# First loads from two queues in chunks of four batches, and masked values written by ScalarE straight from PSUM

## What is computed

```python
x = x + _L0_xattn_ref(_layernorm(x, axis=-1), ctx_768, wq, bq, wk, bk, wv, bv, wo, bo)
# in it, 16 heads of 8 features
q = (x @ wq + bq); k = (y @ wk + bk); v = (y @ wv + bv)
attn = softmax(q k^T / sqrt(8)); out = attn v
return out @ wo + bo
```

## Time and profile before

| | us |
|---|---|
| median of 3 runs | 555.57 (554.25 to 555.69) |
| the profiled execution | 554.04 |
| its span, from the first to the last instruction | 552.2 |
| TensorE busy in the span | 499.0 (90%) |
| VectorE / ScalarE / GpSimd busy | 397.7 / 269.5 / 254.7 |

### The profile page before, as it was taken

One profiled execution on the slowest core, in us unless ns is written; L12 is line 12 of the kernel. 1 busy time (PEld: TensorE's weight loads), 2 busy tenths in 40 slices (PEclk: granted clock), 3 DMA queues, 4 the chain that ended last, 5 costly groups with the idle time before them and its releaser, 6 DMA issues.

```text
span 552.2 us, 13385 instructions
## 1 busy us (share of the span) xinstructions
PE 499.0 (90%) x5113; PEld 380.0 (69%) x5113; DVE 397.7 (72%) x1065; ACT 269.5 (49%) x724; POOL 254.7 (46%) x345
## 2 busy tenths in 40 slices
PE   1698989788999998999989999899878899999996
PEld 1556666545667776877767877788646797798884
DVE  3578888757587789877897879978975578534443
ACT  1355564354476754556646567565543444413331
POOL 3877676215446425556255555334230980084400
PEclk9999999999999999999999999999999999999999
DMA  6900000000001101111000000022201200010001
GB/s 176 244 13 2 4 1 4 2 2 7 3 2 31 31 2 31 31 31 31 2 1 2 3 4 2 2 59 59 60 1 37 78 2 2 0 42 1 2 2 39
DMA packets 21807, 14.47 MB, mean 26 GB/s; under 512 B 5864, under 2 KB 21072, under 8 KB 21744
## 3 DMA queue, kind: packets, MB, share of 16 engines
q1 hardware_dynamic: 21744, 13.61, 9.3%
HBM read 12.30 MB, written 1.05 MB: 24 GB/s over the span
## 4 chain that ended last, share of the span: by engine, by line
PE 69%; DVE 21%; ACT 4%; issue 3%; DMA 1%; SPq 1%; POOL 0%; DVEq 0%; ACTq 0%
PE bank L1681 9%; PE bank L1296 6%; PE bank L1690 5%; PE bank L1452 4%; PE bank L1412 4%; PE bank L1365 4%; PE bank L1432 4%; PE bank L1459 4%; PE bank L1440 4%; PE bank L1621 4%; PE bank L1697 3%; PE bank L1423 3%; PE bank L1282 3%; ACT work L1025 2%; PE bank L1510 2%
## 5 line engine op out<-in xcount | busy, mean ns | idle before, releaser
L478 POOL TENSOR_TENSOR work<-work,rsum 128x496 f32<-128x496 f32 x64 | 64.1, 1014 | 131.1 <-DVE rsum L745 131.1
L1084 ACT ACTIVATE work<-bank,negmax 128x124 f32<-128x124 f32 x256 | 72.7, 378 | 78.5 <-DVE ipa_s L731 78.5
L513 POOL TENSOR_SCALAR work<-work,slot 128x128 f32<-128x128 f32 x64 | 49.8, 792 | 47.6 <-DVE slot L820 31.0
L959 DVE SCALAR_TENSOR_TENSOR work<-work,bank 128x256 f32<-128x256 f32 x64 | 26.9, 420 | 39.5 <-ACT work L1225 39.3
L1681 PE MATMUL bank<-work 128*128 128x256 f32 x224 | 53.5, 382 | 1.4 <-DVE work L962 1.4
L461 POOL TENSOR_TENSOR work<-work 128x512 f32<-128x512 f32 (+2 forms) x48 | 40.2, 837 | 14.1 <-DVE work L701 11.6
L737 DVE COPY work<-bank 128x512 f32<-128x512 f32 x64 | 43.6, 682 | 2.0 <-PE bank L1423 2.0
L1225 ACT ACTIVATE work<-bank 128x256 f32<-128x256 f32 x64 | 24.5, 384 | 41.2 <-PE bank L1681 30.2
L1681 PEld LDWEIGHTS bank<-work 128*128 128x128 f32 x224 | 40.3, 190 | 6.2 <-issue 1.6
L410 POOL TENSOR_TENSOR rstd<-veps,minus_half 128x1 f32<-128x1 f32 (+4 forms) x26 | 20.3, 781 | 51.7 <-DVE veps L555 51.7
L599 DVE TENSOR_REDUCE negmax<-bank 128x8 bf16<-128x1024 f32 x32 | 39.1, 1221 | 5.2 <-PE bank L1267 5.0
(11 more groups left out here) (196 smaller groups left out, 1106.7 us busy)
## 6 DMA issues: line engine op xcount, KB each, us to landing
work<-in_L_ffn_w_dram SPq DMA_DIRECT2D x42, 128.0 KB, 2.3
out_dram<-x_all SPq DMA_DIRECT2D x4, 256.0 KB, 2.5
x_all<-in_x_dram SPq DMA_DIRECT2D x1, 768.0 KB, 6.4
ctx_all<-in_L_ffn_w_dram SPq DMA_DIRECT2D x6, 128.0 KB, 2.2
ctx_all<-in_ctx_dram SPq DMA_DIRECT2D x1, 576.0 KB, 8.2
work<-in_L_xattn_Wq_dram SPq DMA_DIRECT2D x1, 512.0 KB, 8.9
...
```

The source lines that it names most:

```text
L478: pool.tensor_tensor(part, part, rsum1[:, b % 2, CH * n:CH * n + CH].unsqueeze(2).broadcast_to((128, CH, ORG)), ALU.mult).then_inc(Z.norm, 1)
L513: ins = pool.tensor_scalar(ohw_of(e)[:, k, :], count[:, :], slot[:, h, 0, k, e % E1:e % E1 + 1], slot[:, h, 1, k, e % E1:e % E1 + 1], ALU. ...
L1084: ins = act.activation(p1[:, b % 2, n, c, 0:ORG], blocks(bank[n])[:, c, 0:ORG], ACT.Exp, bias=negmax1[:, b % 2, CH * n + c:CH * n + c + 1])
```

## The change

It does three things in the first attention.

- **Loads.** x and context come in four chunks of four batches, in turn, on SyncE's queue, each with semaphores of its own. ScalarE issues the nine loads of the first attention's weights on its queue, in another order, before its table load; the six that the projections need count on a semaphore `qkv0`, the other three on `attn0`. The statistics go by four batches, in rounds -3, -2 and -1, and so do GpSimd's powers.
- **Products.** The two products leave the head of TensorE's program and stand behind round -3. VectorE takes them behind its round -3, and GpSimd adds the bias from round -2 on, behind the masks.
- **Masked values.** VectorE clears `vm0` once. ScalarE's copy of v goes from PSUM straight into the blocks of `vm0` that are not zero (`own_blocks`: 4 x 4 blocks of 8 columns per partition). `v0T` and GpSimd's multiply are gone; who waited for `v_sb` waits for `vm`.

```diff
@@ -106,14 +106,15 @@
-        work = Arena("work", 42000)
+        work = Arena("work", 42032)
         xn = sb("xn", [128, 2, D])
         xT = sb("xT", [128, 2, 128])
         cT_all = sb("cT_all", [C, B, 128])
         qm0 = work.take([128, 4, CH, 128])
         p0T = work.take([128, 2, CH, CH, 128])
-        vm0 = work.take([128, 5, CH, 128])
+        vm_flat = work.take([128, 5 * CH * 128 + 32])
+        vm0 = vm_flat[:, 0:5 * CH * 128].rearrange("p (s g n) -> p s g n", s=5, g=CH)
         km0 = work.take([128, 3, CH, 128], BF16)
...
@@ -283,6 +284,12 @@
+        def own_blocks(c):
+            at = CH * 128 * (c % 5)
+            wide = vm_flat[:, at:at + CH * (128 + D0)].rearrange("p (g n) -> p g n", g=CH)
+            return wide[:, :, 0:128].rearrange("p g (i n) -> p g i n", i=4)[:, :, :, 0:D0]
         def rw2_of(b):
...
@@ -323,20 +330,10 @@
         def _(sp):
-            def load(first, end, x_done, ctx_done):
-                sp.dma_start(x_all[:, first:end, :], T["x"][first:end, :, :].rearrange("b s d -> s b d")).then_inc(x_done, 16)
-                sp.dma_start(ctx_all[:, first:end, :], T["ctx_768"][first:end, :, :].rearrange("b s c -> s b c"))\
-                    .then_inc(ctx_done, 16)
-            load(0, 4, got.x0, got.ctx0)
-            sp.dma_start(wq0[:, :], T["L0_xattn_wq"]).then_inc(got.attn0, 16)
-            sp.dma_start(wk0[:, :], T["L0_xattn_wk"]).then_inc(got.attn0, 16)
-            for bias, name in ((bq0, "L0_xattn_bq"), (bk0, "L0_xattn_bk"), (bv0, "L0_xattn_bv")):
-                sp.dma_start(bias[:, :], T[name].rearrange("(p a) -> p a", a=1)).then_inc(got.attn0, 16)
-            sp.dma_start(wv0[:, :], T["L0_xattn_wv"]).then_inc(got.attn0, 16)
-            sp.dma_start(wo0[:, :], T["L0_xattn_wo"]).then_inc(got.attn0, 16)
-            sp.dma_start(gate_in[:, :], T["L0_ffn_gate_w"]).then_inc(got.attn0, 16)
-            sp.dma_start(bias0[:, :], T["L0_xattn_bo"].rearrange("(a n) -> a n", a=1).broadcast_to((128, D))).then_inc(got.attn0, 16)
-            load(4, B, got.x, got.ctx)
+            for n in range(4):
+                part = slice(4 * n, 4 * n + 4)
+                sp.dma_start(x_all[:, part, :], T["x"][part, :, :].rearrange("b s d -> s b d")).then_inc(x_in[n], 16)
+                sp.dma_start(ctx_all[:, part, :], T["ctx_768"][part, :, :].rearrange("b s c -> s b c")).then_inc(ctx_in[n], 16)
             for w, rows, name in ((wq1, D, "Wq"), (wk1, C, "Wk"), (wv1, C, "Wv")):
...
@@ -424,21 +421,17 @@
             pool.wait_ge(made.masks, 1)
-            pool.wait_ge(made.bias, 1)
             pool.wait_ge(made.cols, 2 * CH)
             def round0(b):
                 a, c = b + 4, b + 3
-                if b == -3:
-                    rstds(4, B)
+                if -3 <= b <= -1:
+                    rstds(4 * (b + 4), 4 * (b + 5))
                 if b == 0:
                     pool.wait_ge(A.cT, 4)
                     pool.tensor_copy(ctx_ipaT[:, :].rearrange("p (b j) -> p b j", b=B), cT_all[:, :, ORG:S]).then_inc(W.ctx, 1)
                 if b in (6, 10, 14):
                     rstds(b - 6, b - 2)
-                if there(a):
-                    pool.wait_ge(A.xn, a + 1)
-                    pool.tensor_tensor(x_all[:, a, :], x_all[:, a, :], bias0[:, :], ALU.add).then_inc(A.xb, 1)
                 if there(c):
...
@@ -448,10 +441,12 @@
                                        ALU.mult).then_inc(A.qm, 1)
-                    pool.wait_ge(A.v_sb, c + 1)
-                    after(pool, A.pv, c - 4)
-                    pool.tensor_tensor(vm0[:, c % 5, :, :], v0T[:, c % 2, :].unsqueeze(1).broadcast_to(wide0), own_col[:, :, :],
-                                       ALU.mult).then_inc(A.vm, 1)
+                if b == -2:
+                    pool.wait_ge(made.bias, 1)
+                for n in (0, 1, 2) if b == -2 else (a,) if b > -2 and there(a) else ():
+                    pool.wait_ge(A.xn, n + 1)
+                    pool.tensor_tensor(x_all[:, n, :], x_all[:, n, :], bias0[:, :], ALU.add).then_inc(A.xb, 1)
             def experts_sum(g):
...
@@ -561,7 +556,8 @@
                 return variances(ln.stats, end, first, end)
-            first_statistics(0, 4, got.x0)
+            dve.memset(vm_flat[:, :], 0.0).then_inc(made.vm, 1)
+            first_statistics(0, 4, x_in[0])
             dve.wait_ge(made.hmask, 3)
...
@@ -577,13 +573,22 @@
             xn0_of(0)
-            dve.wait_ge(got.attn0, 16 * 9)
-            dve.tensor_copy(bv0_wide[:, :], bv0[:, :].broadcast_to((128, 128))).then_inc(made.bias_w, 1)
-            dve.wait_ge(made.bias_p, 1)
-            dve.tensor_tensor(bias0[:, :], OUT0[:, 0:D], bias0[:, :], ALU.add).then_inc(made.bias, 1)
-            dve.wait_ge(F.gate_tr, 1)
-            dve.tensor_copy(gateT[:, :], MAX0[:, 0, 0:E0]).then_inc(F.gateT, 1)
+            def product_input():
+                dve.wait_ge(got.qkv0, 16 * 6)
+                dve.tensor_copy(bv0_wide[:, :], bv0[:, :].broadcast_to((128, 128))).then_inc(made.bias_w, 1)
+            def products_taken():
+                dve.wait_ge(got.attn0, 16 * 3)
+                dve.wait_ge(made.bias_p, 1)
+                dve.wait_ge(F.gate_tr, 1)
+                dve.tensor_tensor(bias0[:, :], OUT0[:, 0:D], bias0[:, :], ALU.add).then_inc(made.bias, 1)
+                dve.tensor_copy(gateT[:, :], OUT0[:, D:D + E0]).then_inc(F.gateT, 1)
             dve.wait_ge(made.consts, 2)
+            rstd_at = {}
...
@@ -612,8 +617,8 @@
                 n, m, t, y = b + 1, b + 2, b - 1, b - 2
-                if b == -3:
-                    rest = first_statistics(4, B, got.x)
+                if -3 <= b <= -1:
+                    rstd_at["first", b] = first_statistics(4 * (b + 4), 4 * (b + 5), x_in[b + 4])
                 if b < FILL:
...
@@ -637,8 +642,8 @@
                     dve_stats(dve, A, y)
-                if b == -3:
-                    dve.wait_ge(ln.rstd, rest)
+                if b <= -2 or b % 4 == 3 and b < 8:
+                    dve.wait_ge(ln.rstd, rstd_at["first", (b + 1) // 4 - 3] if b > -2 else 1)
                 if there(b + 5):
...
@@ -930,6 +934,10 @@
                 round0(b)
+                if b == -4:
+                    product_input()
+                if b == -3:
+                    products_taken()
                 if b in (5, 9, 13, 17):
...
@@ -998,14 +1006,23 @@
         def _(act):
+            for w, name in ((wk0, "wk"), (wq0, "wq"), (wv0, "wv")):
+                act.dma_start(w[:, :], T["L0_xattn_" + name]).then_inc(got.qkv0, 16)
+            for bias, name in ((bk0, "bk"), (bq0, "bq"), (bv0, "bv")):
+                act.dma_start(bias[:, :], T["L0_xattn_" + name].rearrange("(p a) -> p a", a=1)).then_inc(got.qkv0, 16)
+            act.dma_start(wo0[:, :], T["L0_xattn_wo"]).then_inc(got.attn0, 16)
+            act.dma_start(gate_in[:, :], T["L0_ffn_gate_w"]).then_inc(got.attn0, 16)
+            act.dma_start(bias0[:, :], T["L0_xattn_bo"].rearrange("(a n) -> a n", a=1).broadcast_to((128, D))).then_inc(got.attn0, 16)
             act.preload_act_table(ACT.Exp)
-            act.wait_ge(got.attn0, 16 * 9)
+            act.wait_ge(made.vm, 1)
             def round0(b):
                 a, c, n = b + 4, b + 3, b + 4
                 if n < 4:
                     act.wait_ge(A.ctx_tr, n + 1)
                     act.activation(cT_all[:, 4 * n:4 * n + 4, :], blocks(SC0[:, n, :], C), ACT.Copy).then_inc(A.cT, 1)
+                if c == 0:
+                    act.wait_ge(got.qkv0, 16 * 6)
                 if there(c):
...
@@ -1016,8 +1033,9 @@
                     act.activation(q0_bf[:, c % 3, :], TURN0[:, 128:256], ACT.Identity, bias=bq0[:, :]).then_inc(A.q_bf, 1)
-                    after(act, A.vm, c - 1)
-                    act.activation(v0T[:, c % 2, :], TURN0[:, 384:512], ACT.Copy).then_inc(A.v_sb, 1)
+                    after(act, A.pv, c - 4)
+                    act.activation(own_blocks(c), TURN0[:, 384:512].rearrange("p (i g d) -> p g i d", i=4, g=CH), ACT.Copy)\
+                        .then_inc(A.vm, 1)
                 if there(b):
...
@@ -1253,7 +1271,7 @@
-                pe.wait_ge(got.ctx0 if n == 0 else got.ctx, 16)
+                pe.wait_ge(ctx_in[n], 16)
                 for k in range(4):
...
@@ -1311,10 +1329,12 @@
                 after(pe, A.xT, min(a, B))
-                after(pe, A.v_sb, min(c, B))
+                after(pe, A.vm, min(c, B))
                 if there(a):
                     pe.wait_ge(A.xn, a + 1)
                     pe.transpose(TURN0[:, 0:128], xn_in[:, a % 3, :], ident[:, :]).then_inc(A.tr, 1)
+                if c == 0:
+                    pe.wait_ge(got.qkv0, 16 * 6)
                 if there(c):
...
@@ -1620,16 +1640,16 @@
                     mm.then_inc(Z.proj, 1)
-            pe.wait_ge(got.attn0, 16 * 9)
-            pe.wait_ge(made.bias_w, 1)
-            pe.matmul(OUT0[:, 0:D], bv0_wide[:, :], wo0[:, :], start=True, stop=True).then_inc(made.bias_p, 1)
```

(18 more changed lines are left out.)

9 lines of the change are left out of this document (4 added, 5 removed).

## The result

| | before | after |
|---|---|---|
| median of 4 runs, us | 555.63 (554.25 to 556.56) | 548.87 (548.65 to 549.96) |
| the profiled execution / its span, us | 554.04 / 552.2 | 549.04 / 547.3 |
| TensorE busy in the span, us | 499.0 (90%) | 501.2 (92%) |
| VectorE / ScalarE / GpSimd busy, us | 397.7 / 269.5 / 254.7 | 399.9 / 269.8 / 235.2 |

The ratio is 0.9888, with an interval from 0.9861 to 0.9915. The forecast was 549.3 us. The medians differ by 6.8 us, the two profiled executions by only 5.0, and that gap turns out to be worth a look.

The account below looks back on a forecast made before the run. The prediction took TensorE to bound the kernel nearly everywhere except the start-up, where late loads do; 6.45 - 0.35 + 0.2 = 6.3 us off the median of 555.57 gave 549.3 us, range 547.2 to 551.6.

Parts of the forecast that it names:

- Term 1: Start-up: with earlier loads, batch 0's projection starts at 9.4 instead of 15.85, 6.45 us earlier.
- the bound of 1.4 us for a locked-out GpSimd: Start-up: upper bound on the delay if VectorE's new memset kept GpSimd from its constants and first power.
- the sign that I had set: Start-up: a wait of TensorE or VectorE for x, context or weights after 8 us would show the first term wrong.
- Term 2: Between first and second projection: the products, a context turn and a transpose there give 0.35 us back.
- Term 3: Normalisation on VectorE beside GpSimd's masks: GpSimd freed of the masked values makes it 0.2 us earlier.
- Term 4: The rounds: less GpSimd work and ScalarE's masked write change nothing; rounds stay at 5.60 us.
- All later work moves up whole: After the start-up: later work waits for earlier work, not for a date, so the whole gain is kept.
- rival B: TensorE's clock reaches its faster level a round later or earlier: 1.5 us each way, 550.8 or 547.8; chance 0.10 each.
- My last sign: Whole kernel: the forecast is wrong if the start gains 6 us and later phases give them back.
- Rivals A: Start-up loads: shared DMA engines are the limit, a second queue helps less; gain 4.4, 551.2 us; chance 0.13.
- D: Start-up: the last weight load lands 8 us later and holds the products; no gain, 555.6 us; chance 0.04.

Follow-up runs that it names:

- e1_gpsimd_masks: The changed kernel with GpSimd making the masked values again, loads and products kept as changed: 554.46 us, ratio 0.9987.
- e6_three_copies: The changed kernel with three more unread 512-element copies per batch on ScalarE behind its masked write: 549.30 us, ratio 0.9895.
- e8_filler: The changed kernel with ten unread dummy matmuls in TensorE's idle gap of round 13: 548.44 us, ratio 0.9865.
- e2: The kernel before with only the masked values changed (ScalarE writes them, VectorE clears the buffer first): 555.89 us, ratio 0.9995.
- e4: The changed kernel with the two products back at the head of TensorE's and VectorE's programs, behind all nine weight loads: 553.72 us, ratio 0.9949.
- e5: The changed kernel, two queues, but x and context of batches 4 to 15 in one load each: 552.23 us, ratio 0.9949.
- e3: The changed kernel with all loads on SyncE's queue, the nine weight loads behind the first chunk: 549.30 us, ratio 0.9897.
- e7: The changed kernel with six more unread 512-element copies per batch on ScalarE: 567.28 us, ratio 1.0219.
- e10: The changed kernel with the expert block's four normalisations made one by one in rounds 8 to 11: 545.45 us, ratio 0.9809.

## Why the prediction was right

**Term 1, 6.45 us: size right, 0.46 too small; one date wrong.** The projection started at 8.94, not 9.4. x came 0.25 us later than before (I took 0.5), the clearing took 2.22 us (2.2 from the cast's rate), and GpSimd wrote its constants at their old dates beside it, so the bound of 1.4 us for a locked-out GpSimd fell away. But one of its dates was wrong, and by the sign that I had set (a wait of TensorE or VectorE for a load after 8 us) the term fails: I had the weights landed by some 7.3, and bv came at 8.92, with VectorE waiting for it 1.57 us. Context and bv each made TensorE wait, 0.44 and 0.23 us. What made up for this is that batch 0 was transposed earlier than I put it (from 7.19, not 7.4), and that the context turn kept the next matmul away for 0.88 us from start to start and not 1.06. The Trainium skill's cycle per element (VectorE: DVE Perf Modes, Zero memsets can be issued as uint32) had given 2.7 us as an estimate for the clearing; the trace shows 2.22.

**Term 2, 0.35 back: wrong, it was nothing.** From first to second projection there are 3.41 us, and there were 3.40. I added durations of neighbours (1.49 + 0.97 + 1.06 + 0.24), but rows of TensorE overlap at their ends. From start to start the same four steps are 1.44, 0.88, 0.88 and 0.21: half of the error is the context turn (11.26 to the transpose at 12.14), a quarter the products (10.38 to 11.26). The steps should be taken from start to start.

**Term 3, 0.2: size right, reason too small.** The lead grew by 0.28 between the third and fourth projection; the normalisation of batch 4 took 0.51 us (20.74) instead of 0.94. But `e1_gpsimd_masks` shows what stands behind it: without the freed GpSimd the lead at the values is 3.52 us and not 7.69. I had seen the lock and priced it from a GpSimd with gaps, as before had them. The edits were additive in my sum, and they are not.

**Term 4, nothing in the rounds: right**, by the windows of 5.60 us and by `e6_three_copies`.

**"All later work moves up whole": failed** in the profiled execution, by 2.8 us in round 13. This was rival B's mechanism in a place where I hadn't looked. Its first half, the clock rising earlier relative to the work (at 25.3 us, where before, 7.2 us behind, has it at 33.4), gave 0.47 (7.22 to 7.69), a third of the 1.5 that I set. My last sign, that the start gains 6 us and later phases give them back, came true for 2.8 of 7.7.

**The number.** The start gave 7.7 us where I summed 6.3, the clock took 2.8 in one execution, and the median of four came out 6.8 lower. Each of the four has a mean granted clock below 1 (0.979 to 0.994), so each had some stretch at the lower level; where, only the profiled one tells. That 549.3 met 548.87 owes something to luck, to these two misses of opposite sign. Rivals A and D showed themselves with these loads in one profile only, that of `e8_filler`, and in small.

**The falls of the clock.** Of the nine kernels that have the 2.51 us gap in round 13, the granted clock fell behind it in the profiled execution of five (the change, `e1`, `e2`, `e4`, `e5`) and not in four (before, `e3`, `e6`, `e7`); of the four kernels without the gap it fell there in none, but two of these (`e8`, `e10`) lost as much in two falls behind 125 us. In the change, `e2`, `e4` and `e5` it cost 2.78 to 2.79 us each time, in `e1` 1.64. The scatter of before's own runs, 553.54 to 557.91 us over 25, is of that size, and it goes with the clock: of the 55 executions of before beside the experiments, the 17 with a mean granted clock of 0.997 or more took 553.7 to 554.7 us, the other 38 took 552.7 to 558.2. The Trainium skill (TensorE: Matmul & The Clock Gate, Part 1) says of a kernel's start that the point at which the upper level begins varies from run to run of one kernel. The scatter of one kernel's runs fits that, but only one execution of each was profiled, so no pair of traces here shows it. Which execution is hit, and whether the date of the gap has a part in it, stays open: each kernel has one profile, and that is too few.
